# Hybrid transformer layer on one core: first values after one rotation less, second group's rows in two parts over two queues, maxima turned ahead of the next pieces

## What is computed

```python
x = x + attn_a(layernorm(x), wq, wk, wv, wo)     # 32 heads of 16, rotary, causal softmax
x = x + ffn(layernorm(x), ...)                   # base matrix + top-2 of 8 rank-16 experts
x = x + attn_b(layernorm(x), Wq, Wk, Wv, Wo, ..) # 32 query heads of 128, 8 key heads, RMS norm, ALiBi
x = x + ffn(layernorm(x), ...)                   # same weights as the first
```

## Time and profile before

| | us |
|---|---|
| median of 3 runs | 1540.65 (1540.48 to 1541.16) |
| profiled execution, its own time | 1541.88 |
| its span | 1540.1 |
| TensorE busy in the span | 1484.7 (96%) |
| VectorE busy | 1101.3 (72%) |
| ScalarE busy | 801.0 (52%) |
| TensorE's granted clock, mean | 0.994 |

### The profile page before, as it was taken

How to read it: one execution, slowest core, us unless ns; L and a number is a source line. 1 busy time by engine, 2 the same in 40 slices (tenths; PEclk the granted TensorE clock), 3 DMA queues, 4 the chain that set the end, 5 groups by cost and what they waited for, 6 DMA issues and landing times.

```text
span 1540.1 us, 25370 instructions
## 1 busy us (share of the span) xinstructions
PE 1484.7 (96%) x8968; PEld 1168.1 (76%) x8968; DVE 1101.3 (72%) x2792; ACT 801.0 (52%) x2095; POOL 431.7 (28%) x424
## 2 busy tenths in 40 slices
PE   7999999997998999999999999999999999999997
PEld 5754444444877888888888888888888888888776
DVE  5687787742767876776787687677678768767873
ACT  6515666564235555555555555545555554555441
POOL 4102000022634412231341241333134134134332
PEclk9999999998999999999999999999999999999999
DMA  4556333310201001000100100100010010010000
GB/s 156 148 100 93 47 43 43 43 57 8 69 1 41 17 12 35 8 28 1 42 28 1 42 22 7 42 8 21 1 42 28 1 41 22 8 35 8 8 21 28
DMA packets 40205, 54.26 MB, mean 35 GB/s; under 512 B 5776, under 2 KB 21392, under 8 KB 40080
## 3 DMA queue, kind: packets, MB, share of 16 engines
q1 hardware_dynamic: 40080, 52.65, 14.4%
HBM read 44.04 MB, written 8.39 MB: 34 GB/s over the span
## 4 chain that ended last, share of the span: by engine, by line
PE 70%; DVE 3%; issue 1%; ACT 1%; POOL 1%; POOLq 0%; DVEq 0%; ACTq 0%
PE ps L50 20%; PE ps L52 19%; PE ps L51 19%; PE ps L1664 8%; PE ps L1639 2%; PE ps L246 0%; DVE prob L1915 0%; PE ps L1641 0%; DVE ab_pt_l L1933 0%; ACT ab_squares L1809 0%; DVE ab_xt_l L256 0%; PE ps L1441 0%; DVE f1n_stats L221 0%; ACT ab_xt_h L251 0%; DVE ab_qt_l L1924 0%
## 5 line engine op out<-in xcount | busy, mean ns | idle before, releaser
L1797 ACT ACTIVATE prob<-prob,ab_neg_max 128x128 f32<-128x128 f32 (+7 forms) x256 | 201.4, 787 | 252.7 <-DVE ab_neg_max L1915 251.4
L1933 DVE TENSOR_TENSOR ab_pt_l<-ps,ab_pt_h 128x512 fp32r<-128x512 f32 x288 | 198.0, 688 | 66.9 <-ACT ab_pt_h L1825 65.1
L1825 ACT CAST ab_pt_h<-ps 128x512 fp32r<-128x512 f32 x288 | 171.8, 596 | 123.3 <-PE ps L1664 122.5
L474 DVE TENSOR_REDUCE ra_part_max<-ps 128x1 f32<-128x512 f32 (+3 forms) x304 | 183.1, 656 | 51.9 <-PE ps L467 34.5
L1915 DVE CUSTOM_DVE_ANT_0 prob<-ps,rel 128x512 f32<-128x512 f32 (+3 forms) x256 | 146.2, 571 | 101.3 <-PE ps L52 100.0
L1547 POOL TENSOR_TENSOR ab_rms<-ab_ms_eps,neg_half 128x5 f32<-128x5 f32 x64 | 77.3, 1207 | 397.1 <-DVE ab_ms_eps L1958 397.0
L50 PE MATMUL ps<-ab_w_h,ab_xt_h 128*128 128x512 f32 (+1 forms) x512 | 182.6, 357 | 1.7 <-DVE ab_v_l L1953 1.7
L1941 DVE TENSOR_SCALAR prob<-prob,ab_recip 128x128 f32<-128x128 f32 (+7 forms) x256 | 167.1, 653 | 9.1
L1664 PE MATMUL ps<-ident,prob 128*128 128x128 f32 x1152 | 173.4, 273 | 0.0
L52 PE MATMUL ps<-ab_w_h,ab_xt_l 128*128 128x512 f32 (+1 forms) x512 | 172.7, 337 | 0.0
L51 PE MATMUL ps<-ab_w_l,ab_xt_h 128*128 128x512 f32 (+1 forms) x512 | 172.3, 336 | 0.0
(11 more groups left out here) (225 smaller groups left out, 3378.3 us busy)
## 6 DMA issues: line engine op xcount, KB each, us to landing
f_raw<-in_wqkv SPq DMA_DIRECT2D x32, 384.0 KB, 3.7
f_raw<-in_wbo SPq DMA_DIRECT2D x32, 256.0 KB, 2.6
ra_first_rows<-parts SPq DMA_DIRECT2D x36, 128.0 KB, 6.7
parts<-pa_stage SPq DMA_DIRECT2D x12, 256.0 KB, 3.0
parts<-f_raw SPq DMA_DIRECT2D x12, 256.0 KB, 3.5
ra_q_st<-parts SPq DMA_DIRECT2D x24, 128.0 KB, 6.5
ra_k_st<-parts SPq DMA_DIRECT2D x24, 128.0 KB, 6.6
f_raw<-in_wf SPq DMA_DIRECT2D x8, 324.0 KB, 3.4
```

Of the source, the lines that this page charges most:

```text
L474: return dve.tensor_reduce(maxima[:, first:first + heads, i], bank[:, 0:heads * (k1 - k0)].rearrange("p (h k) -> p h k", h=heads), AX.X, A ...
L1797: act.activation(prob[:, t % 2, h, 0:w], prob[:, t % 2, h, 0:w], ACT.Exp, bias=neg_max[:, t % 2, h, pieces_per_head(t % NT) - 1:pieces_per ...
L1825: act.copy(pt_h[:, n % PT, :], ring_bank("p", u, j)).then_inc(pt_high, 1)
L1933: dve.tensor_tensor(pt_l[:, n % PT, :], ring_bank("p", u, j), pt_h[:, n % PT, :].bitcast(F32), ALU.subtract).then_inc(emptied, 1)
```

## The change

Four edits, all in `rotary_projection_block` and the class `FirstMaxima` that it uses:

1. `project_values(0)` waits for seven rotated tiles and no more for eight.
2. The rows of group 1 come in two parts. Columns 0 to 767 (12 transfers of 96 KB) are issued by ScalarE, behind `take_values(1)`, once the loads of pair 0 and the stores of pairs 0 to 2 have landed, and count on `rows_in[0]`. Columns 768 to 1023 (12 of 32 KB) stay where all were, on SyncE behind the loads of pair 3.
3. `score_next` and the end of SyncE's list wait for both parts.
4. `turn_max` and `take_max` stand ahead of pieces 0 and 1 of group 1.

```diff
@@ FirstMaxima.score_next
             if n == 0:
+                pe.wait_ge(self.rows_in[0], 2 * 16 * 2 * len(A_TERMS))
                 pe.wait_ge(self.loaded[1], 16 * 2 * len(A_TERMS))
@@ SyncE
-            first.load_rows(sp, 1, slice(0, T), first.loaded[1])
+            first.load_rows(sp, 1, slice(T - 2 * P, T), first.loaded[1])
             first.store_max(sp)
             sp.wait_ge(first.max_in[0], 16 * A_PARTS)
             sp.wait_ge(first.loaded[1], 16 * 2 * len(A_TERMS))
+            sp.wait_ge(first.rows_in[0], 2 * 16 * 2 * len(A_TERMS))
@@ TensorE
             pe.wait_ge(weights.w_low, 2 * KC)
-            pe.wait_ge(rot_done, NT)
+
+            pe.wait_ge(rot_done, NT - 1)
             project_values(0)
             turn(NT - 1)
             project_values(1)
@@
-            first.score_next(pe, 0, 2)
             first.turn_max(pe)
-            first.score_next(pe, 2, a_pieces_before(A_SHIFT))
+            first.score_next(pe, 0, a_pieces_before(A_SHIFT))
@@ ScalarE
             high(NT - 1)
             mid(NT - 1)
             take_values(1)
+
+            act.wait_ge(first.rows_in[0], 16 * 2 * len(A_TERMS))
+            act.wait_ge(stored[1], 16 * 6)
+            act.wait_ge(stored[0], 16 * 6 * 2)
+            first.load_rows(act, 1, slice(0, T - 2 * P), first.rows_in[0])
             for i in range(2, NT):
                 take_values(i)
@@ VectorE
             first.split_max(dve)
-            first.max_of_next(dve, 0, 2)
             first.take_max(dve)
-            first.max_of_next(dve, 2, a_pieces_before(A_SHIFT))
+            first.max_of_next(dve, 0, a_pieces_before(A_SHIFT))
```

## The result

| | us |
|---|---|
| before, median of 14 runs | 1539.38 (1538.02 to 1541.16) |
| after, median of 14 runs | 1544.07 (1542.4 to 1546.96) |
| ratio after / before | 1.0028, 95% interval 1.0021 to 1.0035 |
| span of the profiled execution after | 1544.3 |

The change makes the kernel slower by 0.28%, or 4.3 us (3.2 to 5.4); the medians differ by 4.7. The forecast was +6.1.

A forecast was written before the change was run, and what follows sets the result against it. TensorE, busy 96% of the span, was taken as the bound. Terms: -1.1 (first edit) + 6.7 (stores held up) + 1.4 (clock) - 0.9 (end) = +6.1 us, median 1540.65 to 1546.75, range 1538.6 to 1549.9.

The forecast's parts named there:

- First edit, 2.3 us won and 1.1 left by pair 3's rows: TensorE's pieces start 2.3 us sooner, but piece 22 waits for pair 3's rows until 94.2, leaving 1.1 us.
- The loads hold up the stores: ScalarE's group 1 loads delay SyncE's stores for pair 3; a delay of 3.6 us or more had chance 0.57.
- By 6.7 us: Delay of pair 3's stores: 9.4 us of engine time for ScalarE's loads at 126 GB/s, less 2.7 idle.
- Start of the transfers: On ScalarE's queue, 12 transfers issued from 76.7 us until 82.2, their data starting at about 77.9.
- Pair 2's rows: nothing on the path: Pair 2's rows land some 3 us later, at about 84.5, when TensorE reaches piece 11, at no cost.
- Piece 22 later by 5.6: Pair 3's rows land at 100.9, so TensorE starts piece 22 5.6 us later than at 95.29.
- Clock, 1.4: After TensorE's long idle before piece 22 the granted clock drops to 0.5, costing 1.4 us.
- End, -0.9, and the order's own price of about 1.0: Group 1's first reduction starts sooner, 0.9 us won; the new order alone costs about 1.0 against the old with rows in time.
- Rival 1: Queues don't hold each other up: stores' delay 0 to 3.5 us, change -2.0 to +1.5 us; chance 0.31.
- Rival 2: First edit's gain kept whole, pair 3's rows in by 93.0: -3.2 us, time 1537.4; chance 0.04.
- Rival 3: ScalarE's queue bounds, issues of 1.0 us or more delaying tile 2's copy: +1.6 us, 1542.3; chance alone 0.08.
- the likeliest case: Pair 3's stores held up by 3.6 us or more: +3.1 us and up, 1544.5 to 1549.9; chance 0.57.

The follow-up runs named there:

- e9_narrow: Kernel before plus the first edit and 12 added 96 KB transfers on ScalarE's queue, each into 16 partitions, SyncE still loading everything: 1.0033 of the kernel before.
- e5_halves: Kernel before plus the first edit, old order; group 1's rows come in two halves on SyncE, its first piece waiting for the first only: 0.9986.
- e4_thin: Kernel before plus the first edit and 12 added ScalarE transfers of 64 columns (8 KB each), SyncE still loading everything: 1.0002 of the kernel before.
- e7_behind_stores: Changed kernel in the old order, ScalarE issuing its 12 loads behind the copy of tile 3, once pair 3's stores have landed: 1.0051 of the kernel before.
- e8_halves_early_stores: e5_halves with pair 3's four high and middle stores issued by ScalarE behind the copy of tile 1: 0.9978 of the kernel before, median 1537.12 us.
- e1_first_wait: Kernel before with the first edit alone, project_values(0) waiting for seven rotations: 1.0003 of the kernel before.
- e2_split_alone: Kernel before with the split load alone (second and third edit): 1.0006 of the kernel before.
- e6_halves_turn_first: e5_halves with edit 4, the turn ahead of pieces 0 and 1 of group 1: 0.9985 of the kernel before.
- e10_wide: e9_narrow with ScalarE's 12 transfers of 96 KB spread over 96 partitions, with stand-in data: 1.0011 of the kernel before.
- e3_old_order: Changed kernel with only edit 4 undone, pieces 0 and 1 of group 1 ahead of the turn again: 1.0034 of the kernel before.

## Why the forecast was right, and where its sizes were off

- **First edit, 2.3 us won and 1.1 left by pair 3's rows.** Right. From `turn(6)` to the first piece it takes 7.66 us, 10.14 before, so 2.5. Alone, the edit wins nothing that can be told, since group 1's rows take the last 1.1 too. This I had left unsaid, as the split comes with it.
- **The loads hold up the stores.** Right, and this is the step that decides. It is shown by the thin and the full transfers at the same place: SyncE's stretch +0.3 and +5.3.
- **By 6.7 us.** Too much: 4.3, and up to 5.3 in the other two traces of the same traffic. The term that was mis-sized is the engines' time for ScalarE's loads, 9.4 us at 126 GB/s. The DMA view of the stretch, before (73.83 to 87.31) and then after (73.35 to 91.10), has it:

```profile
q1 hardware_dynamic: 4128, 1.97, 52.8%
```

```profile
q1 hardware_dynamic: 4128, 1.97, 48.3%
q10 hardware_dynamic: 960, 1.18, 33.2%
```

  33.2% of 17.75 us is 5.9 (7.2 in `e9_narrow`). The bytes are the forecast's 1.18 MB, but 126 GB/s is what such loads reach when only such loads are in flight. In the view from 80.3 to 84.4, beside pair 2's loads, ScalarE's 0.42 MB take 69.2% of 4.1 us, which is 148 GB/s of engine time. From 84.4 to 91.2, beside the stores, its 0.36 MB take 16.2% of 6.8 us, 327 GB/s. The idle share that they fill was put at 2.7 and is 3.1 (6.3 before, 3.2 after). One term was put at nothing: SyncE's own packets take 8.6 us and not 7.1, 1.5 more. Together 5.9 + 1.5 - 3.1 = 4.3.
- **Start of the transfers.** ScalarE's first issue was at 75.06, forecast for 76.7, so the loads met pair 2's from the start.
- **Pair 2's rows: nothing on the path.** Nearly: they landed at 85.2, forecast for 84.5, and TensorE was at piece 11 at 84.0 and waited 1.20 us. This wait is then swallowed by the one at piece 22, which is shorter for it.
- **Piece 22 later by 5.6.** From `turn(6)` it is 30.70 us after, 27.60 before: 3.1. The wait in front of it was 4.08 us, where 6 to 9 were named as the sign.
- **Clock, 1.4.** It was 1.6: from piece 22 to the chain 12.15 us after and 10.56 before. The window behind the wait has the clock at its low level:

```profile
98.00:101.50 3.50, 3.46 (x9) 2.15 (x9) 1.79 (x3) 0.00 (x0) 0.00 (x0) 0.51 0.24 69
```

- **End, -0.9, and the order's own price of about 1.0.** Both right inside the block: 0.98 and 0.98. In the times neither the old order on the changed kernel nor the new order on `e5_halves` makes a difference that can be told. I let everything behind the block move as it was, and in the trace 0.9 us were added there. They go with a longer stretch at the low clock (the last section has the rows of all traces), and whether this kernel has it in most executions is not known from one trace.
- **Rival 1, no holding up,** is out by `e4_thin` against `e9_narrow`, and by `e7_behind_stores`. **Rival 2** asked for SyncE sooner, which `e8_halves_early_stores` gives, and then the time does fall. **Rival 3** came in part: the ten issues after the first copy took 7.08 us and not 4.6, 0.71 each where the rival asks for 1.0. The copy of tile 2 ended 1.6 us before its bank was needed, and 1.2 of that was TensorE's wait at piece 11.

By its measured terms the sum is 3.1 (piece 22) + 1.6 (clock) - 1.0 (end) + 0.9 (behind the block) = +4.6 us, against 4.3 (3.2 to 5.4) by the ratio. That the total comes this near the forecast's 6.1 is luck in part: the 0.9 behind the block was not in it. The range given for the likeliest case alone, 1544.5 to 1549.9, starts higher than its own condition, since +3.1 on 1540.65 is 1543.75. The measured 1544.07 lies between the two, and the three runs that the forecast started from were 1.3 us above the median of 14.

## What to carry to other kernels

A load that leaves a busy queue for an idle one still uses the same DMA engines; before moving it forward, list what the first queue has in flight at the new time and which wait hangs on it, and add both queues' bytes at the rate that such loads reach together. If the aim is only that a consumer starts sooner, let it wait for the part that it reads, on the queue that is there. An edit that removes a wait wins nothing until the next data that its engine needs comes sooner as well, so follow the engine to its next wait before counting the gain.

## What was not expected of the hardware

- Loads into 16 partitions at a time did not go faster for being on two queues. Alone on one queue they moved 126 GB/s with the engines full; on two queues it was 121 GB/s at a share of 1.13 (`e9_narrow`) and 115 GB/s (`e7_behind_stores`, 87 to 101.5 us). With one of the two queues spread over 96 partitions it was 205 GB/s at 0.75. With only such loads in flight, 12 transfers of 32 KB, which land 6.9 us after the first issue when alone (estimate from the earlier trace rows), made a piece wait 9.8 us.
- Ten DMA issues on ScalarE took 7.08 us with 96 KB each and 6.40 us with 8 KB each, where SyncE takes 4.6 for ten in a row. Neither the size nor a full set of DMA engines explains it: in `e7_behind_stores` ScalarE issued the same 12 loads in 5.60 us from 86.75 on, 0.47 each. A stretch with few issues appears on both queues at about 76 us in the changed kernel (ScalarE has three in 3.05 us from 75.96, SyncE four in 3.39 us from 75.59), and a shorter one on SyncE alone in `e1_first_wait` (two in 2.11 us from 76.22). Its cause stays open.
- How long the low clock lasts behind the block differs from trace to trace, and the time to the second group's chain goes with it:

| kernel | clock at 0.5 behind the block's last reduction, us | from there to the second group's chain, us |
|---|---|---|
| before | 3.4 | 21.68 |
| `e9_narrow` | 3.4 | 21.70 |
| `e1_first_wait` | 3.7 | 21.60 |
| `e2_split_alone` | 4.0 | 21.75 |
| `e7_behind_stores` | 4.6 | 22.04 |
| changed | 5.8 | 22.59 |
| `e5_halves` | 5.8 | 22.61 |
| `e8_halves_early_stores` | 6.2 | 22.81 |
| `e6_halves_turn_first` | 6.5 | 22.93 |
| `e10_wide` | 6.5 | 22.95 |
| `e3_old_order` | 6.6 | 22.99 |
| `e4_thin` | 6.7 | 23.03 |

  Each us at the low clock goes with about 0.4 us. It does not go with what was won or lost ahead of it: slow `e9_narrow` has as little as the kernel before, and `e4_thin`, which is as fast as that one, has the most. So 1.4 us of any difference between two single traces can be this.
